# Gate products from the residual stream in a fused transformer block with experts

## The reference

```python
h = h + attn(layernorm(h))            # 16 heads of 64, output product 1024 -> 256, bias l_b
xt = layernorm(h)                     # (x - m) / sqrt(v + eps), no gain, no bias
logits = xt @ w_g                     # w_g is 256 x 8
top_v, top_i = top_k(logits, 2)
probs = softmax over the two chosen   # so: exp of the gap between them
# rank of each choice within its expert, in order of rows; those over capacity are dropped
h = h + sum over chosen experts of prob * (gelu(xt @ c_fc[e]) @ c_proj[e])
```

## Time and profile before

| what | value |
|---|---|
| median of 3 runs | 774.4 us (773.43 to 774.83) |
| profiled execution | 771.51 us, its span 769.7 us |
| PE busy | 693.9 us (90% of the span) |
| DVE busy | 514.1 us (67%) |
| ACT busy | 293.2 us (38%) |
| POOL busy | 281.5 us (37%) |
| chain that ended last | PE 81%, DVE 8%, issue 4%, ACT, DMA and POOL 2% each |

### The profile page before, as it was taken

How to read it: one execution, slowest core, us unless ns; L and a number is a source line. 1 busy time by engine, 2 the same in 40 slices (tenths; PEclk the granted TensorE clock), 3 DMA queues, 4 the chain that set the end, 5 groups by cost and what they waited for, 6 DMA issues and landing times.

```text
span 769.7 us, 16733 instructions
## 1 busy us (share of the span) xinstructions
PE 693.9 (90%) x6527; PEld 651.6 (85%) x6527; DVE 514.1 (67%) x1143; ACT 293.2 (38%) x652; POOL 281.5 (37%) x293
## 2 busy tenths in 40 slices
PE   5989998999989999899997861599999999999995
PEld 4878888888989889898986751499999999999995
DVE  4994575887868778687877834275664747567471
ACT  3545543544534345343542211243342524334240
POOL 3573100013040220403003044526666565666606
PEclk9998999999999999999998565599999999999998
DMA  8640000001000010000000014224444543544212
GB/s 274 165 132 21 2 2 1 17 2 31 1 18 16 3 30 2 18 16 7 26 2 26 8 30 161 69 73 91 125 99 100 105 81 84 97 130 88 39 14 29
DMA packets 51265, 42.99 MB, mean 56 GB/s; under 512 B 25383, under 2 KB 44757, under 8 KB 51201
## 3 DMA queue, kind: packets, MB, share of 16 engines
q1 hardware_dynamic: 21729, 30.20, 12.5%
q0 software_dynamic: 29472, 11.90, 9.7%
HBM read 32.76 MB, written 10.25 MB: 56 GB/s over the span
## 4 chain that ended last, share of the span: by engine, by line
PE 81%; DVE 8%; issue 4%; ACT 2%; DMA 2%; POOL 2%; POOLq 0%; SPq 0%; DVEq 0%; ACTq 0%
PE pair L1314 12%; PE pair L1316 11%; PE pair L1315 11%; PE shared L1314 9%; PE shared L1315 8%; PE shared L1316 8%; PE ct_ps L1439 5%; PE pair L1429 5%; PE vt_ps L1416 3%; DVE top L1020 1%; DVE expo L1023 1%; PE ct_ps L1338 1%; DVE zsum L1029 1%; DMA token_rows<-sent 1%; ACT ctx_hi L795 1%
## 5 line engine op out<-in xcount | busy, mean ns | idle before, releaser
L715 POOL DMA_INDIRECT out<-yrow,held x48 | 100.9, 2102 | 74.4 <-DVE yrow L1276 60.3
L887 ACT ACTIVATE act_f<-pair 128x348 f32<-128x348 f32 (+1 forms) x128 | 51.8, 457 | 97.5 <-PE pair L1316 97.5
L1314 PE MATMUL pair<-xe_hi,fc_hi 128*128 128x348 f32 (+1 forms) x256 | 82.7, 323 | 1.1 <-DVE xe_lo L1258 1.1
L1316 PE MATMUL pair<-xe_hi,fc_lo 128*128 128x348 f32 (+1 forms) x256 | 83.2, 325 | 0.0
L1315 PE MATMUL pair<-xe_lo,fc_hi 128*128 128x348 f32 (+1 forms) x256 | 83.0, 324 | 0.0
L698 POOL DMA_INDIRECT held<-token_rows,found_ix x48 | 68.3, 1422 | 26.3 <-issue 19.4
L1314 PE MATMUL shared<-pj_hi,act_hi 128*116 128x256 f32 (+1 forms) x256 | 72.2, 282 | 0.0
L1316 PE MATMUL shared<-pj_hi,act_lo 128*116 128x256 f32 (+1 forms) x256 | 71.9, 281 | 0.0
L1315 PE MATMUL shared<-pj_lo,act_hi 128*116 128x256 f32 (+1 forms) x256 | 71.8, 281 | 0.0
L791 ACT ACTIVATE expo<-expo 69x552 f32<-69x552 f32 x64 | 42.4, 662 | 72.4 <-DVE expo L1023 72.3
L777 ACT ACTIVATE qkv<-shared,bq_sb 128x276 f32<-128x276 f32 x99 | 48.2, 487 | 45.2 <-PE shared L1316 45.2
(11 more groups left out here) (217 smaller groups left out, 1995.3 us busy)
## 6 DMA issues: line engine op xcount, KB each, us to landing
raw_fc<-c_fc SPq DMA_DIRECT2D x8, 1024.0 KB, 7.2
raw_pj<-c_proj SPq DMA_DIRECT2D x8, 1024.0 KB, 7.3
qkv<-w_qkv SPq DMA_DIRECT2D x6, 512.0 KB, 7.3
qkv<-patches SPq DMA_DIRECT2D x6, 384.0 KB, 4.8
token_rows<-sent POOLq DMA_DIRECT2D x8, 285.7 KB, 7.1
out<-h SPq DMA_DIRECT2D x8, 276.0 KB
more_patches<-patches SPq DMA_DIRECT2D x3, 384.0 KB, 8.8
qkv<-w_l SPq DMA_DIRECT2D x1, 1024.0 KB, 7.3
```

The costliest lines, as they stand in the source:

```text
L715: pool.indirect_dma_start(out, bass.IndirectOffsetOnAxis(ap=xg[p][0:n, t, D:D + 1].bitcast(U32), axis=0), yrow[p][0:n, t, :], None, bounds ...
L887: gelu = act.activation(act_f[f % 2][:, a:b], pair[f % 2][:, h, 0:b - a], ACT.Gelu)
L1314: pe.matmul(dst, l_hi, r_hi, start=(first and n == 0), stop=False)
L1316: done = pe.matmul(dst, l_lo, r_hi, start=False, stop=(last and n == len(terms) - 1))
```

## The change

The normalised rows are not transposed for the gate any more. Since (x - m) r W = r x (W - mean of W over its rows), the gate products are taken from the residual stream itself with weights that are centred once, and the scale r is applied to the gap of the two best logits.

- `project_out` adds the input rows on PE: behind each block of 24 matmuls come three float32 matmuls of `rows` (92 x 128 weights) with the identity (92 columns). Its result, with the bias, is the residual stream and is called `hT` in place of `yT`.
- `turn_y` transposes `hT`; on DVE `take_rows` copies it to `h2`, where `residual` added.
- `turn_x2`, `put_x2T` and the two bank uses "x2t" of each group are gone. `logit` uses `hT` and `wg_mid`.
- Once, in group 0, unit 1: `average_gates` (two float32 matmuls) and `middle_gates` (a DVE subtraction, behind `take_max` of unit 2) make `wg_mid`, by a new bank use "mean". POOL fills `part_of` once at the start.
- POOL multiplies the gap by `m_rs`; `put_gap` waits for that. `norm_mid` waits until the multiplication of the group before is done.
- In the tail PE's order is now `tabulate` of group 6, `project_out`, `logit`, `turn_y`, `count`, `tabulate` of group 7. DVE picks first, then `take_rows`, `norm_mid`, `put_place`, `norm_mid_end`. POOL does `spread` ahead of `store_x2` for the last group.

```diff
-    for g in range(GROUPS + 1):
+    for g in range(GROUPS):
         for u in range(UNITS):
             order += group_uses(g, u)
-    order += [("table", GROUPS - 1, 0)]
+    g = GROUPS - 1
+    order += [("table", g - 1, 0), ("proj", g, 0), ("proj", g, 1), ("logit", g, 0), ("ytr", g, 0), ("ytr", g, 1),
+              ("rank", g, 0), ("table", g, 0)]
...
-                 4: [("x2t", g - 1, c) for c in range(KD)],
...
+    if g == 0 and u == 1:
+        uses += [("mean", 0, 0)]
...
                 pool.tensor_tensor(gap[:, :], best[:, 1, :], best[:, 0, :], ALU.subtract).then_inc(s_gap, 1)
+                wait(pool, s_gap, st, lambda i: 2 * (i + shift) + 1)
+                pool.tensor_tensor(gap[:, :], gap[:, :], m_rs[:, :], ALU.mult).then_inc(s_gap, 1)
...
             weigh(Step(GROUPS), -1)
+            spread(Step(GROUPS), -1)
             store_x2(Step(GROUPS), -1)
-            spread(Step(GROUPS), -1)
...
+            def middle_gates():
+                bank, nth = USE[("mean", 0, 0)]
+                dve.wait_ge(s_full[bank], nth)
+                dve.tensor_tensor(wg_mid[:, :, :], wg_sb[:, :, :],
+                                  shared[bank][:, 0:NEXP].unsqueeze(1).broadcast_to([128, KD, NEXP]), ALU.subtract)\
+                    .then_inc(s_wg_mid, 1)
+                dve.wait_ge(s_wg_mid, 1)
+                dve.sem_inc(s_free[bank], 1)
...
-                    dve.tensor_tensor(h2[:, a:b, :], shared[bank][0:TR, 0:(b - a) * D].rearrange("p (t d) -> p t d", d=D),
-                                      src, ALU.add).then_inc(s_free[bank], 1)
+                    dve.tensor_copy(h2[:, a:b, :], shared[bank][0:TR, 0:(b - a) * D].rearrange("p (t d) -> p t d", d=D))\
+                        .then_inc(s_free[bank], 1)
...
             add_table(last, -2)
-            residual(last, -1)
-            norm_mid(last, -1)
-            norm_mid_end(last, -1)
             put_logits(last, -1)
             pick(last, -1, 0)
             pick(last, -1, 1)
+            take_rows(last, -1)
+            norm_mid(last, -1)
             put_place(last, -1)
+            norm_mid_end(last, -1)
...
             def project_out(st, shift):
                 wait(pe, s_c_lo, st, lambda i: UNITS * (i + shift + 1))
+                wait(pe, s_h, st, lambda i: i + shift + 1)
                 for c in range(KD):
                     bank = free(st, "proj", shift, c)
                     w = slice(c * 128, (c + 1) * 128)
                     three(shared[bank][:, 0:GT], [(wl_hi[:, k, w], wl_lo[:, k, w], ctx_hi[:, k, :], ctx_lo[:, k, :])
-                                                  for k in range(PAIRS)]).then_inc(s_full[bank], 1)
+                                                  for k in range(PAIRS)], last=False)
+                    for t in range(TPG):
+                        done = pe.matmul(shared[bank][:, t * TR:(t + 1) * TR], rows[:, (st.i + shift) * TPG + t, w],
+                                         ident[0:TR, 0:TR], start=False, stop=(t == TPG - 1))
+                    done.then_inc(s_full[bank], 1)
...
             last = Step(GROUPS)
+            tabulate(last, -2)
             project_out(last, -1)
-            tabulate(last, -2)
+            logit(last, -1)
             turn_y(last, -1)
-            turn_x2(last, -1)
-            logit(last, -1)
 
             count(last, -1)
             tabulate(last, -1)
```

More of the change, by code:

```diff
@@ L802, in put_y @@
                     wait(act, s_full[bank], st, nth)
-                    act.activation(yT[:, c, :], shared[bank][:, 0:GT], ACT.Identity,
+                    act.activation(hT[:, c, :], shared[bank][:, 0:GT], ACT.Identity,
                                    bias=bl_sb[:, c:c + 1]).then_inc(s_free[bank], 1)
             def put_gap(st, shift):
-                wait(act, s_gap, st, lambda i: i + shift + 1)
+                wait(act, s_gap, st, lambda i: 2 * (i + shift + 1))
                 act.activation(e_gap[:, :], gap[:, :], ACT.Exp).then_inc(s_egap, 1)
[L811 to L815, removed]
             act.wait_ge(s_const, 48)
@@ L829, in stage_b @@
                     blocks = list(qkv_of(u)) if more else []
-                    if u == 4 and before:
-                        put_x2T(st, -1)
                     ahead = 3 if u == 1 else 2
@@ L1192, in stage_b @@
                         take_max(Step(st.i + 1, st.k, st.span), 0)
+                    if u == 1 and st.i == 0:
+                        middle_gates()
                     if u == 7 and before:
@@ L1448, in project_out, with average_gates @@
                     three(shared[bank][:, 0:GT], [(wl_hi[:, k, w], wl_lo[:, k, w], ctx_hi[:, k, :], ctx_lo[:, k, :])
-                                                  for k in range(PAIRS)]).then_inc(s_full[bank], 1)
+                                                  for k in range(PAIRS)], last=False)
[3 more added lines that the diff above has]
+                    done.then_inc(s_full[bank], 1)
+            def average_gates():
+                bank = free(Step(0), "mean", 0, 0)
+                pe.wait_ge(s_part_of, 1)
+                for c in range(KD):
+                    done = pe.matmul(shared[bank][:, 0:NEXP], part_of[:, :], wg_sb[:, c, :], start=(c == 0), stop=(c == KD - 1))
+                done.then_inc(s_full[bank], 1)
             def turn_y(st, shift):
-                ready(st, "proj", "ytr", shift)
+                taken(st, "proj", shift, range(KD))
                 for n, tiles in enumerate((range(1), range(1, TPG))):
@@ L1457, in turn_y @@
                             at = (t - tiles[0]) * D + c * 128
[L1458 to L1467, removed]
+                            done = pe.transpose(shared[bank][0:TR, at:at + 128], hT[:, c, t * TR:(t + 1) * TR], ident[:, :])
                     done.then_inc(s_full[bank], 1)
             def logit(st, shift):
-                ready(st, "x2t", "logit", shift)
+                taken(st, "proj", shift, range(KD))
                 bank = free(st, "logit", shift, 0)
@@ L1474, in logit @@
                     for c in range(KD):
-                        done = pe.matmul(shared[bank][0:TR, t * NEXP:(t + 1) * NEXP], x2T[:, c, t * TR:(t + 1) * TR],
-                                         wg_sb[:, c, :], start=(c == 0), stop=(c == KD - 1))
+                        done = pe.matmul(shared[bank][0:TR, t * NEXP:(t + 1) * NEXP], hT[:, c, t * TR:(t + 1) * TR],
+                                         wg_mid[:, c, :], start=(c == 0), stop=(c == KD - 1))
                 done.then_inc(s_full[bank], 1)
@@ L1530, in stage_b @@
                         tabulate(st, -2)
+                    if u == 1 and st.i == 0:
+                        average_gates()
                     if u == 0 and more:
                         turn_x(st, 1, range(1))
-                    if u == 4 and before:
-                        turn_x2(st, -1)
                     if u == 5 and before:
```

21 lines of the change are left out of this document (10 added, 11 removed).

## The result

The changed kernel takes 792.65 us (791.76 to 794.97, 6 runs), the one before 773.91 us in the same session (773.25 to 775.58, 6 runs): ratio 1.0242, 95% interval 1.0223 to 1.0262. Forecast were 790.5 us in 783 to 799. The profiled execution took 793.09 us, span 791.3, against 769.7 before: 21.6 us more, while the medians differ by 18.7, because the profiled execution of before lay 2.4 us under its median and that of after 0.4 above it.

What follows compares the result with a forecast made beforehand. PE was taken to bound the loop, the order of waits the tail. Loop +7.8, group 0 +1.5 and tail +6.8 sum to +16.1 us: profiled 771.5 to 787.6, plus 2.9 for the median, 790.5 us, range 783 to 799.

Steps and rivals of the forecast that it cites:

- the loop: All groups' added row matmuls less the removed transposes on PE: 6 x 1.05 + 1.5 = +7.8 us (4.0 to 14.1).
- Row matmuls, 1.5 us a group: PE in the loop: 12 new float32 records at 0.124 us each, 1.5 us a group, between 0.96 and 2.4.
- the rival with 0.201: New matmuls' load and stream follow one another, 0.201 us a record: loop +14.1, whole 797.7 us; chance 0.20.
- the estimate in the prediction: Skill's isolated-matmul price, N / 2.4 + 2.5 ns: 0.041 us for 92 columns, loop +0.7; rejected for 0.124 a record.
- Transposes, -0.45 us a group: PE in the loop: dropping six transposes saves 0.62 + 0.15 - 0.32 = 0.45 us a group.
- The last step, +1.5: Loop's last step: no q, k, v products left, PE behind DVE, transpose saving hidden, so row matmuls count fully, +1.5 us.
- Group 0, +1.5: Group 0, unit 1: bank of average_gates released late, context 2.7 us late, partly taken back; +1.5 us (0.8 to 2.7).
- PE's clock behaves otherwise behind the idle stretch: Stated sign of being wrong; forecast had PE's clock low again after about 7 us idle before the tail's project_out.
- The tail, +6.8: After the last context: PE idles for in_spot, project_out and store late; store lands at 483.7, +6.8 us (+4.0 to +11.8).
- The freed bank uses: Two bank uses fewer per group in the loop: could only help where PE waits for a bank; no saving counted.
- The rival on the faster side: Two bank uses less per group remove PE's loop waits, 24.4 us at most: 766.1 us; chance 0.03.

Runs made afterwards that it cites:

- the filled wait: Changed kernel with 11 float32 identity products into unused PSUM where PE waits for the bank in group 0, unit 1: 789.57 us, ratio 1.0211.

## Why the prediction was right, point by point

The direction held, the median lies in the range, and of the terms the loop was the largest, as forecast, with the tail next. (The prediction's text calls the tail the largest single term; its own sum, 7.8 against 6.8, has it the other way.) How near the median came is luck in part. The profiled difference of 21.6 us stands against a sum of 16.1: group 0 is 2.2 us dearer, the loop 3.0, the tail 0.3 cheaper, and 0.6 lies outside all terms. The median came within 2.2 us of the forecast because the 2.9 us by which the profiled execution of before lay under its median was added, and did not recur: the profiled execution of after lies 0.4 us above its median.

- **Row matmuls, 1.5 us a group: a little too dear.** Measured 1.3, from three group periods. With 0.11 us a record the weight load of the gate products, scaled, was a fair bound from above, and load and stream do overlap: the rival with 0.201 is out. The Trainium skill's figure for an isolated matmul ("TensorE: Matmul & The Clock Gate", Back-to-back issue gap), 0.041 by the estimate in the prediction, is 2.7 times too low here.
- **Transposes, -0.45 us a group: this step failed in part.** They give 0.15. The chain did run through them, but without them DVE's `expo` of that unit comes 0.24 us too late for the next scores. The step took "a group thus saves" 0.45 from the matmuls alone, and did not look at what PE asks for next. Both errors nearly cancel, which is luck too: net 1.05 forecast, 1.14 measured, and for all of the loop 7.8 against 8.2.
- **The last step, +1.5**: measured +1.35 behind the last mark, and +0.8 in the step before it.
- **Group 0, +1.5: the term that was mis-sized most.** It was +3.7. The bank's wait was where it was forecast (2.43 us; the block begins 29.8 us behind stage B's first product, for which 30.2 was forecast, and the context 2.4 us later than before, for which 2.7 was). The delay alone, by the filled wait, costs about 1.0 and so lies in the stated 0.8 to 2.7. But the prediction put the clock behind the wait at nothing, and that is about 3.0.
- **The clock in the loop, 2.6 us in this profile: not in the prediction, and its cause stays open.** "PE's clock behaves otherwise behind the idle stretch" was thought of for the tail alone.
- **The tail, +6.8**: measured +6.5. `project_out` started 7.0 us later than before, as forecast. It then took 8.9 us and not 9.7, since the lower clock lasted 2.8 us from its start and not 4.5; the forecast also had 3.7 us for the last 28 matmuls, where its rows give 453.98 - 450.1 = 3.9. Against that, from the gap to the store it took 5.92 us and not 5.45: POOL's multiplication of 92 x 3 took 0.91 us, beside DVE's `in_row`. The copies on DVE cost 0.41 and 0.68 us, just like the additions.
- **The freed bank uses**: nothing. The waits for `table` are 1.3 us as before, and the two uses brought back cost no more than their transposes. The rival on the faster side is out.

**Why the change costs time, then.** An addition that DVE made at no cost to the end, since it is not what sets the loop's pace and its copy takes as long, was moved to the engine that does set it, for 1.3 us a group. What was removed there was partly hidden. The shorter way to the gate only pays where nothing covers it, in the last group, and there the order of the queues ate it.

## What to carry to other kernels

When work moves between engines, price it by what sets the pace in each stage, and make it stage by stage: here the same edit loses 8 us in the loop and, with the order mended, gains 3.4 in the tail. For work removed from the bounding engine, look at the next thing it asks for; the saving ends there. Price a new wait on PE together with the clock behind it, and see whether an independent piece of work can stand in the wait. And before reading a difference of one or two microseconds out of a stage, look at how long the lower clock lasts at its start in either profile.

## What was not expected of the hardware

- A wait of 2.43 us in group 0 was followed by 6.85 us at the lower clock, from 92.0 to 98.85 us, although PE was busy throughout; in two of the seven profiles with this wait it was 3.4 us. Waits of 1.28 us in the loop were followed by a fall in some groups and by none in others, 11 times in 52 over all profiles. The Trainium skill ("TensorE: Matmul & The Clock Gate", The HAM clock gate) lets the clock follow how busy PE has been recently; that filling the wait kept it at 1.00 agrees with that.
- POOL's product of two 92 x 3 tiles took 0.19 us at 456.95 and 0.91 us at 485.61, where DVE ran `in_row` (92 x 696, 0.88 us) from 485.58 on. The other profiles show the same: the product takes 0.91 us in each of the ten in which it stands beside `in_row`, and 0.19 to 0.24 everywhere else. POOL's pair of 92 x 24 products takes 1.13 to 1.16 us wherever it overlaps `in_row`, in all 14 profiles, and 0.41 to 0.46 where it doesn't. So the step of POOL that stands beside this operation of DVE is 0.7 us longer, and the order of the work decides which step that is. Why, and whether other operations of DVE do the same, was not tried.
